# Turning the row maxima of an attention kernel: by a transposing DMA instead of TensorE and ScalarE, with a lead of 112 units

## The reference, cut to what matters

```python
left = x[..., :E // 2]                       # N=16, S=1024, E=256, H=16, Dh=8
q = (left @ Wq.T).reshape(N, S, H, Dh)       # k and v likewise
energy = jnp.einsum('nqhd,nkhd->nqkh', q, k)
att = jax.nn.softmax(energy / scale, axis=2)
out = jnp.einsum('nqkh,nkhd->nqhd', att, v)
...
x = x + _layernorm(attention(_layernorm(x)))
# gf: a small net on the mean over the sequence; 3 cycles of:
tf = _coupling_net(out)                      # 256->256->128->64->1, GELU, GELU, GELU, sigmoid
coupling = 0.1 + adaptive_range * (0.7 * gf + 0.3 * tf - 0.5) * 2.0
out = out + coupling * _twist(out)
...
x = x + _layernorm(coupled(_layernorm(x)))
```

## Time and profile before

| | |
|---|---|
| median of 3 runs | 3677.8 us |
| the profiled execution, its own time | 3678.55 us |
| its span in the trace | 3676.5 us |
| TensorE matmul busy | 94% |
| VectorE busy | 83% |
| ScalarE busy | 81% |
| GpSimd busy | 24% |
| TensorE clock granted, mean | 0.973 |

### The profile page before, as it was taken

One profiled execution on the slowest core, in us unless ns is written; L12 is line 12 of the kernel. 1 busy time (PEld: TensorE's weight loads), 2 busy tenths in 40 slices (PEclk: granted clock), 3 DMA queues, 4 the chain that ended last, 5 costly groups with the idle time before them and its releaser, 6 DMA issues.

```text
span 3676.5 us, 56241 instructions
## 1 busy us (share of the span) xinstructions
PE 3441.4 (94%) x20096; PEld 1018.6 (28%) x20096; DVE 3033.7 (83%) x5740; ACT 2983.7 (81%) x4028; POOL 874.5 (24%) x1258
## 2 busy tenths in 40 slices
PE   3998999999999999999999999999999999999996
PEld 1222232322323232232322323232232323223232
DVE  3998979888898888889888898888889888898922
ACT  2776969798897978979798897978879798896974
POOL 2003040320504123050311405023050411404033
PEclk6998999999999999999999999999999999999998
DMA  3111112021120302112021210302112030111001
GB/s 69 34 27 38 22 37 33 25 46 26 45 27 24 54 17 51 28 42 33 24 48 24 50 22 26 53 17 56 27 43 29 24 52 19 38 22 35 2 24 35
DMA packets 48405, 123.69 MB, mean 34 GB/s; under 512 B 13568, under 2 KB 14976, under 8 KB 40064
## 3 DMA queue, kind: packets, MB, share of 16 engines
q1 hardware_dynamic: 44960, 101.74, 13.9%
q0 software_dynamic: 2304, 16.78, 2.5%
q10 hardware_dynamic: 864, 1.57, 0.3%
HBM read 34.61 MB, written 33.55 MB: 19 GB/s over the span
## 4 chain that ended last, share of the span: by engine, by line
PE 65%; DVE 14%; ACT 12%; issue 5%; POOL 2%; DMA 1%; SPq 0%; ACTq 0%; POOLq 0%; DVEq 0%
PE heads_ps L420 22%; PE ring_ps L381 14%; DVE max_parts L833 11%; PE scoresT_ps L405 9%; PE scoresT_ps L518 8%; ACT p_sb L607 4%; PE scoresT_ps L523 3%; PE ring_ps L449 2%; PE scoresT_ps L526 1%; ACT headsT L616 1%; ACT x_in L620 1%; DVE stats L844 1%; DMA k_rows<-parts 1%; ACT parts L660 1%; PE scoresT_ps L464 1%
## 5 line engine op out<-in xcount | busy, mean ns | idle before, releaser
L833 DVE TENSOR_REDUCE max_parts<-ring_ps 128x1 f32<-128x512 f32 x3708 | 2354.2, 684 | 305.5 <-PE ring_ps L381 259.7
L607 ACT ACTIVATE p_sb<-scoresT_ps 128x1024 f32<-128x1024 f32 x2048 | 1987.6, 1024 | 193.0 <-PE scoresT_ps L405 166.8
L381 PE MATMUL ring_ps<-k_rows,q_rows 48*128 48x512 bf16 x3708 | 1101.9, 388 | 44.3 <-DVE max_parts L833 30.4
L420 PE MATMUL heads_ps<-p_sb,v_sb 128*9 128x512 f32 x8192 | 1085.6, 602 | 16.9 <-ACT headsT L616 11.7
L405 PE MATMUL scoresT_ps<-q_rows,k_rows 51*128 51x512 bf16 x4096 | 1042.7, 387 | 14.8 <-ACT p_sb L607 6.6
L381 PEld LDWEIGHTS ring_ps<-k_rows,q_rows 48*128 48x128 bf16 x3708 | 274.8, 94 | 1286.8 <-DVE max_parts L833 1121.4
L984 POOL CAST max_split<-max_all 128x16 bf16<-128x16 f32 x128 | 25.1, 196 | 1931.5 <-DVE max_all L839 1930.2
L518 PE MATMUL scoresT_ps<-state,w 128*128 128x512 f32 x768 | 382.4, 622 | 7.7 <-issue 4.9
L405 PEld LDWEIGHTS scoresT_ps<-q_rows,k_rows 51*128 51x128 bf16 x4096 | 220.8, 94 | 222.2 <-ACT p_sb L607 174.2
L729 ACT ACTIVATE p_sb<-scoresT_ps,b 128x512 f32<-128x512 f32 x192 | 131.4, 684 | 178.8 <-PE scoresT_ps L518 178.5
L420 PEld LDWEIGHTS heads_ps<-p_sb,v_sb 128*9 128x9 f32 x8192 | 123.5, 88 | 331.3 <-issue 294.0
(11 more groups left out here) (170 smaller groups left out, 2873.8 us busy)
## 6 DMA issues: line engine op xcount, KB each, us to landing
q_rows<-parts SPq DMA_DIRECT2D x186, 128.0 KB
k_rows<-parts SPq DMA_DIRECT2D x186, 128.0 KB
x_sb<-in_x SPq DMA_DIRECT2D x16, 1024.0 KB, 4.7
out<-x_sb SPq DMA_DIRECT2D x16, 1024.0 KB, 3.9
out<-x_in POOLq DMA_DIRECT2D x16, 1024.0 KB, 8.0
x_in<-in_x SPq DMA_DIRECT2D x15, 1024.0 KB, 6.1
q_rows<-neg_rows SPq DMA_DIRECT2D x512, 3.0 KB
x_in<-in_x SPq DMA_DIRECT2D x4, 256.0 KB, 4.0
```

The costliest lines, as they stand in the source:

```text
L381: e.matmul(ring_bank(max_taken, u + 1), q_rows[rows, slot, pair, h * BANK + qb * P:h * BANK + (qb + 1) * P], k_rows[rows, slot, pair, kh * ...
L420: m = e.matmul(heads_ps[32 * j:32 * j + DH + 1, :], v_sb[:, b % 2, kb, 4 * (group % NG) + j, 0:DH + 1], p_sb[:, n % 2, j, :], start=(kb == ...
L607: e.activation(p_sb[:, n % 2, 2 * two:2 * two + 2, :].rearrange("p h n -> p (h n)"), scoresT_ps[:, 2 * two * BANK:(2 * two + 2) * BANK], A ...
L833: e.tensor_reduce(max_parts[:, gi % 2, kh, col:col + 1], bank_of(max_taken, u + 1), AX.X, ALU.max).then_inc(max_taken, 1)
```

## The change

The turn is taken off TensorE and ScalarE. GpSimd cuts the maxima as before, now into the first 48 columns of `max_wide`, a 128 x 128 bfloat16 tile whose other 80 columns are set to zero once. SyncE waits for the cut, issues one transposing DMA from `max_wide` to `max_rows` (both in SBUF), waits until it has landed, and then issues the same four small DMAs, now from `max_rows`. GpSimd's next cut waits for the transposing DMA instead of the matmul. The sign moves into the constant rows: they hold minus one instead of one. The identity in bfloat16 is gone. `LEAD` goes from 104 to 112.

```diff
-TWO_ONES = 1.0 + 16256 * 2.0 ** -23
+MINUS_ONES = -1.0 - 49024 * 2.0 ** -23
-LEAD = 104
+LEAD = 112
-        max_split = sb("max_split", [P, 2 * 2, MROWS, TPH], BF16)
-        neg_rows = sb("neg_rows", [MROWS * MU, P], BF16)
+        max_wide = sb("max_wide", [P, P], BF16)
+        max_split = max_wide[:, 0:MROWS * MU].rearrange("p (s j q) -> p s j q", s=2 * 2, j=MROWS)
+        max_rows = sb("max_rows", [P, 1, P], BF16)
...
# SyncE
             def lay_max_rows(gi):
                 b, h, g = gi // GROUPS, gi % GROUPS // NG, gi % NG
-                e.wait_ge(neg_ready, gi + 1)
+                e.wait_ge(max_cut, gi + 1)
+                if gi == 0:
+                    e.wait_ge(const_dve, 1)
+                else:
+                    e.wait_ge(max_rows_laid, 64 * gi)
+                e.dma_start_transpose(max_rows[:, :, :], max_wide[:, :]).then_inc(max_turned, 16)
+                e.wait_ge(max_turned, 16 * (gi + 1))
                 if b >= 2:
                     e.wait_ge(pv_done, step_of(b - 1, 0))
                 for side in range(2):
                     for two in range(2):
                         at, n = 64 * side + ROWS, MROWS * TPH * (2 * side + two)
                         e.dma_start(q_rows[at:at + MROWS, b % 2, 2 * g + two, h * BANK:(h + 1) * BANK],
-                                    neg_rows[n:n + MROWS * TPH, :]).then_inc(max_rows_laid, 16)
+                                    max_rows[n:n + MROWS * TPH, 0, :]).then_inc(max_rows_laid, 16)
# TensorE
-                    if u >= PER_GROUP and u % PER_GROUP == LAY_AFTER:
-                        turn_max(u // PER_GROUP - 1)
...
-            def turn_max(gi):
-                e.wait_ge(max_cut, gi + 1)
-                ps = misc_bank(neg_ready, gi + 1)
-                e.matmul(ps[0:MU * MROWS, 0:P], max_split[:, :, :, :].rearrange("p s j q -> p (s j q)"),
-                         ident_bf[:, :], start=True, stop=True).then_inc(neg_turned, 1)
# ScalarE
-                        e.wait_ge(neg_turned, gi + 1)
-                        if gi:
-                            e.wait_ge(max_rows_laid, 64 * gi)
-                        e.activation(neg_rows[:, :], bank_of(neg_ready, gi + 1)[0:MU * MROWS, 0:P], ACT.Copy,
-                                     scale=-1.0).then_inc(neg_ready, 1)
# VectorE, once
+            e.memset(max_wide[:, MROWS * MU:P], 0.0)
-                                e.memset(ones_rows(1), TWO_ONES).then_inc(ones_laid, 1)
+                                e.memset(ones_rows(1), MINUS_ONES).then_inc(ones_laid, 1)
# GpSimd
                 e.wait_ge(max_joined, gi + 1)
                 if gi:
-                    e.wait_ge(neg_turned, gi)
+                    e.wait_ge(max_turned, 16 * gi)
...
-            e.memset(ones_rows(0), TWO_ONES).then_inc(const_pool, 1)
+            e.memset(ones_rows(0), MINUS_ONES).then_inc(const_pool, 1)
```

More of the change, by code:

```diff
@@ L124, in attention_ffn_program @@
         ident = sb("ident", [P, P])
-        ident_bf = sb("ident_bf", [P, P], BF16)
         sign = sb("sign", [P, 1])
@@ L153, in attention_ffn_program @@
         rows_q1 = [sem(f"rows_q1_laid{i}") for i in range(2)]
-        max_rows_laid = sem("max_rows_laid")
+        max_turned, max_rows_laid = sem("max_turned"), sem("max_rows_laid")
         scores_done, pv_done = sem("scores_done"), sem("pv_done")
         max_done = [sem(f"max_done{i}") for i in range(2)]
-        neg_turned, xT_done, qk_done, v_done = sem("neg_turned"), sem("xT_done"), sem("qk_done"), sem("v_done")
+        xT_done, qk_done, v_done = sem("xT_done"), sem("qk_done"), sem("v_done")
         headT_done, tokT_done, wo_done = sem("headT_done"), sem("tokT_done"), sem("wo_done")
         yT_done, fin_done, g_done, ffn_done = sem("yT_done"), sem("fin_done"), sem("g_done"), sem("ffn_done")
-        exp_done, heads_evac, neg_ready = sem("exp_done"), sem("heads_evac"), sem("neg_ready")
+        exp_done, heads_evac = sem("exp_done"), sem("heads_evac")
         featx_ready, qk_evac, v_ready = sem("featx_ready"), sem("qk_evac"), sem("v_ready")
@@ L590, in scalar_program @@
         def scalar_program(e):
-            def max_units(done, upto):
-                for u in range(done, upto):
-                    if u >= PER_GROUP and u % PER_GROUP == LAY_AFTER:
-                        gi = u // PER_GROUP - 1
-                        e.wait_ge(neg_turned, gi + 1)
-                        if gi:
-                            e.wait_ge(max_rows_laid, 64 * gi)
-                        e.activation(neg_rows[:, :], bank_of(neg_ready, gi + 1)[0:MU * MROWS, 0:P], ACT.Copy,
-                                     scale=-1.0).then_inc(neg_ready, 1)
             def exp(b, n, two):
@@ L743, in layer_out @@
                         scale_coupling(b, cycle, l)
-            done = 0
             for b in range(-2, N + 2):
@@ L754, in scalar_program @@
                             scale_coupling(b - 2, 2, CYCLE - 1)
-                        upto = units_in_step(b, n, two)
-                        max_units(done, upto)
-                        done = max(done, upto)
                     if valid(b) and n and n % NT == 0:
                         take_heads(b, n - 1)
-                    upto = units_in_step(b, n, 2)
-                    max_units(done, upto)
-                    done = max(done, upto)
                 if valid(b):
@@ L815, in scalar_program @@
                             take_state(b, STATE.index(j))
-                    upto = units_in_beat(b, j)
-                    max_units(done, upto)
-                    done = max(done, upto)
         def vector_program(e):
@@ L1041, in gpsimd_program @@
             e.wait_ge(const_pool, 2)
-            e.tensor_copy(ident_bf[:, :], ident[:, :])
             e.memset(minus_half[:, :], -0.5)
```

## The result

| | before | after |
|---|---|---|
| median (runs) | 3676.4 us (4) | 3631.1 us (4) |
| lowest to highest | 3672.4 to 3679.2 | 3629.6 to 3631.4 |
| the profiled execution, its own time | 3678.55 | 3631.04 |
| its span | 3676.5 | 3629.2 |

The ratio is 0.9875, with a 95% interval of 0.9861 to 0.9889: faster by 45 us. The forecast was 3614 us in a range of 3586 to 3662. The sign is right, and the gain is 17 us short of the 64 that were summed.

A forecast was written before the change was run, and what follows sets the result against it. TensorE was taken as close to the bound nearly everywhere, with all three engines near it in attention. 53.2 + 3.1 + 4 + 7 - 3 = 64.3 us off 3678.55 gave 3614 us, range 3586 to 3662.

The forecast's parts named there:

- The turn in attention: Attention, batches 1 to 14: removing six turns from TensorE and ScalarE gains 3.8 us a stage, 53.2 us in all.
- all joins show: Attention stages: VectorE's six joins of 0.17 us each stay visible, so only 3.3 of 4.3 us are gained.
- none does: Attention stages: none of VectorE's joins lengthens the step, so the full 4.3 us a stage are gained.
- The lead of 112: Batch 0's coupling stage: eight units moved in from batch 15's attention cost 3 us (0 to 5).
- The coupling stages: 14 full coupling stages: TensorE is the bound, two turns of 0.24 us fewer gain 7 us (0 to 21).
- Batch 0: Batch 0's attention, bounded by VectorE: its 4.8 us of waits for TensorE's units shrink, gaining 4 us (0 to 4.8).
- Batch 15: Batch 15's attention: five turns in place of six, so five sixths of a stage's gain, 3.1 us.
- The constants: Start: zeroing 80 columns and writing minus one hide under loads and memsets and cost nothing; uncovered, under 1 us.
- The slower rival: Next batch's row DMAs come too late in attention, stalling TensorE; 3781 us if the transposing DMA takes 19 us; chance 0.07.
- T: SyncE's transposing DMA, time from issue to landing: taken as 3 us (3 to 19), costing nothing up to 7.1.
- The first rival: VectorE's join and ScalarE's exponentials hold the step; only engines' own time returns, 29 us less 3, 3653 us; chance 0.13.
- rows 3: Trace close-up of one turn: cut 1.3 us after the join; TensorE idle 0.54 us, VectorE 0.82, ScalarE 0.52.

The follow-up runs named there:

- dma_lead104: The changed kernel with LEAD at 104 again in place of 112, so the transposing DMA alone; 3616.4 us, ratio 0.9839 to before.
- dma_lead108: The changed kernel with LEAD at 108 in place of 112; 3612.5 us, ratio 0.9830 to before.
- pool_update_first: The changed kernel, LEAD 112, with GpSimd's state update written ahead of the cut of the same step; 3615.8 us, ratio 0.9836 to before.
- pe_lead112: The kernel before, turn still on TensorE, with LEAD at 112 in place of 104; 3737.8 us, ratio 1.0171 to before.
- turn_x3: The changed kernel with each transposing DMA issued three times, each waited for; 3660.9 us, ratio 0.9947 to before.
- turn_x5: The changed kernel with each transposing DMA issued five times, each waited for; 3993.3 us, ratio 1.0853 to before.
- wait_only: The changed kernel at LEAD 104 with TensorE waiting for GpSimd's cut at the turn's old place, without matmul, bank or copy; 3623.0 us, ratio 0.9843 to before.
- copy_only: The changed kernel at LEAD 104 with ScalarE's copy alone put back, from a constant SBUF tile, without matmul or bank; 3615.3 us, ratio 0.9827 to before.

## Why the prediction was right or wrong

**The turn in attention, 3.8 us a stage: mechanism and size right.** In steps 3 to 63 without step 7 the DMA gives 3.9 us a stage at a lead of 104 and 4.0 at 108 and 112. I had set the middle between "all joins show" and "none does". In after a pair with a join takes 4.02 us against 3.97, so little of it shows; VectorE's 3.92 us of work fit into the pair. By whole stages it is 4.0 (dma_lead104), 4.3 (dma_lead108) and 4.4 us (pool_update_first), and the differences between these are the first three steps, which nobody had in the sum.

**The lead of 112, 3 us in batch 0's coupling: the step that failed.** There it costs 2.1 us (53.1 against dma_lead104's 51.0; the other kernels with the DMA and a lead of 104 take 49.3 to 51.4), inside the 0 to 5. The turns' removal took 2.6 us off the same stage (53.6 to 51.0), a gain that I had left out. But I priced the lead only by the units that it moves. It moves the cuts too, and the cut of group 3 came ahead of GpSimd's state update in step 5, which put that update beside VectorE's. This costs 13.5 us in step 7, and putting GpSimd's update first gave 11.7 us of the attention stages back (15.3 by the medians, of which the tail's part is not explained). It is the largest single miss, near the 17 us that the forecast was off, but that is partly luck. The other terms fell short by 16.9 us, in the coupling stages above all, and 13.4 came in beyond the sum: 7.0 in the first three steps, 3.5 in batch 0's coupling and 2.9 by the turn. GpSimd's order around each cut could have been read from the kernel, and both updates read their two inputs from SBUF. I had followed SyncE's queue and TensorE's and left out GpSimd's.

**The coupling stages, 7 us (0 to 21): the lower end.** Nothing was gained at a lead of 104 (+0.5 us in 14 stages) and 3.3 us lost at 112. TensorE is busy 77.9 of 80.9 us there, and still 0.24 us of its work taken off twice a stage is worth nothing. I read this as the chain of the coupling network setting the length, which no run tests. pe_lead112 shows that this hangs on the beat: elsewhere two turns cost 3.2 us a stage ((1173.8 - 1128.4) / 14, both at a lead of 112).

**Batch 0, 4 us (0 to 4.8): the lower end.** I took seven waits of 4.8 us for the turns' because the total matched. They are 5.0 us in seven waits without any turn, five of them at the same places. A total that matches names no cause; the neighbours of one of the waits would have.

**Batch 15, 3.1 us:** 2.5. **The constants:** nothing to be seen; the start is 1.6 us shorter.

**The tail, not in the sum:** +4.1 us. It is 150.9 to 158.3 us in the twelve other executions looked at, in no order with the edits, and follows the granted clock of the tail: 158.3 us at 0.86, 157.5 at 0.87 (after), 153.4 at 0.89 (before), 152.3 at 0.90 (dma_lead104), 150.9 at 0.91. I put it down to the clock; it wasn't tested by itself.

Summed: 3.7 + 0.6 + 3.5 + 10.3 - 3.5 + 2.5 = 17.1 us less gain than forecast, in the order attention, batch 15, batch 0, coupling, batch 0's coupling, and start with tail. In the first of these, 2.9 us of more gain by the turn and 7.0 in the first three steps stand against the 13.5 of step 7.

**The slower rival (T above 7.1 us):** T is 2.3 us, so it didn't come, and turn_x3 and turn_x5 show that its mechanism and its place were right. The Trainium skill's 1309 ns by the crossbar (VectorE: DVE Perf Modes, "The three transpose paths") is not measured by itself here; 2.3 us from issue to landing is in line with it, and T by strides, as that page warns, is ruled out. That the page's DMA way is slower than TensorE's 390 ns also holds here (2.3 us against a matmul and a copy of 0.5 us together) and yet decided nothing, because nobody waits for it.

**The first rival (the step is held by something else, 29 us):** refuted, the pairs have nearly their plain length. **My reading of rows 3** named the wait for the cut, the held bank, and the idle engines in one breath. In steps 3 to 63 of the 14 stages, where the whole turn costs 54.6 us, the wait alone costs 14.7, the copy alone 3.0 and the matmul with its bank 51.9. They don't add up: at steps 30 and 62 the wait alone costs 0.52 us, the matmul with its bank 0.60 and all of it 0.69. So the wait is largely hidden behind what the bank costs already.

## What to carry to other kernels

The price of a small operation on a path of several busy engines need not be its duration or the wait that the trace shows ahead of it. Here most of it came with the matmul and the bank that it took out of a tight ring until another engine gave it back. Put the pieces back one at a time to find which one costs, and compare them step by step: a total of 5 us hid a cost of 14.7. When a lead or a phase changes, follow every queue with an instruction tied to it, and look at what then runs side by side on GpSimd and VectorE with SBUF inputs: here 1 us of collision in each of 14 batches took 12 to 15 of the 61 us that were to be had. A hidden transfer has a margin; adding it two or four times more shows where it ends, and beyond it the price is not linear.

## What the runs showed of the hardware

- VectorE's `tensor_tensor` of 128x512 float32 took 1.79 us beside one of GpSimd's of 1.29 us, and 0.68 us alone.
- A transposing DMA of a 128x128 bfloat16 tile from SBUF to SBUF took 2.3 us from issue to landing and 1.1 us on SyncE's queue; behind row DMAs up to 4.7 us. In turn_x5 SyncE waited up to 11.0 us for one.
- A wait of TensorE's sequencer of 71 us in total (wait_only) cost 0.52 us in each of two places of a stage and nothing in the others, and 128 extra instructions of ScalarE (copy_only) cost nothing that the total shows.
